# A windowed attention and three convolutions on one core: scores ahead of values in TensorE's order, and a shorter opening

## The chip, the cores and the metric

The kernel runs on one core of one Trainium2 chip. Its time is the device time of one execution in microseconds. Of the kernel before there are three runs: 203.22, 203.52 and 203.56 us, median 203.52 us. A further execution was taken with the profiler. All waits between engines are semaphores written out by hand; each engine works through its own list of instructions in order.

## The reference

The input is eight images of 28 x 28 pixels with 64 channels. Four blocks follow each other, each of the form x = x + block(groupnorm(x)), with 32 groups of two channels:

```python
x = x + attention(_gn(x))     # shifted windows 7x7, 8 heads of 8 channels, relative bias, mask, softmax
x = x + binary_conv(_gn(x))   # 3x3, signs of input and kernel, scaled by a 3x3 mean of |input|
x = x + ternary_conv(_gn(x))  # 3x3, kernel = sign
x = x + gated(_gn(x))         # in-projection, causal conv of 4 taps, silu, gate, out-projection
```

The change touches only the first block. For every window and head it computes

```python
attn = einsum('whnd,whmd->whnm', q * scale, k) + relative_position_bias + attn_mask
out  = einsum('whnm,whmd->whnd', softmax(attn), v)
```

and then a projection of 64 to 64 channels.

## The kernel before

**Tiles.** The images are handled in four pairs (g = 0 to 3), one image in partitions 0 to 63 and one in 64 to 127. An image has 4 x 4 windows. A row R = 4g + r (16 in all) is one row of four windows of an image pair. A row is worked on in two steps of two windows each, k = 2R (even) and k = 2R + 1 (odd); the text calls a step a pair of windows, and there are 32.

**One step of the attention.** *seed(k)* (ScalarE, L553) writes relative bias and mask into one of two PSUM pairs, which alternate by step. *scores(k)* (TensorE, L881) adds q times k on top. *shift(k)* (VectorE, L1292 and L1297) takes the maximum and subtracts it. *turn(k, 0)* and *turn(k, 1)* (TensorE, L892) transpose the result, and *expo(k, j)* (ScalarE, L583) takes the exponential. *values(k)* (TensorE, L912) multiplies with v and gives the sums too. After a row, *weigh(R)* (VectorE, L1306 and L1311) divides, *gather(R)* (TensorE, L925) transposes, *evac_att(R)* (ScalarE, L595, four instructions) brings it out of PSUM, *project(R)* (TensorE, L938) projects, and *residual(R)* (VectorE, L1322) adds it to x.

**What a row needs first.** *proj_qk(R)* (TensorE, L852) computes q and k of a row; *evac_qk(R)* (ScalarE, L562 for the keys `ks`, L563 for the queries `qs`) copies them out; GpSimd's *mask_row* (L224) spreads the keys by head into `kex`, one of two buffers. *proj_v(R)* (TensorE, L862) computes v after q and k have been copied out, since it uses the same PSUM bank; *evac_v(R)* (ScalarE, L573, two instructions) copies it. proj_v(R + 1) and evac_v(R + 1) belong to the even step of row R, for R = 1 to 14; in row 0, proj_v(1) is in the odd step.

**The order of TensorE.** It is written out by hand. L954 loops over steps 0 to 29. A step issues turn(k, 0), turn(k, 1); in an even one proj_qk(R + 2) and project(R - 2), in an odd one gather(R - 1); then values(k - 1); in an even one proj_v(R + 1); and last scores(k + 2). In the odd steps of rows 0, 2, 3, 6, 10 and 14 a small matmul follows, a *mix* (L815, L816) of the moments of a normalisation or (row 3) a sum for the binary convolution (L985). Both write a free part of the bank of q and k. From row 2 on they wait for evac_att of the row before. The mix of row 14 belongs to the binary convolution of the third image pair.

**The order of ScalarE** (L621) in step k: expo(k, 0), expo(k, 1); in an even step evac_qk(R + 2), then evac_v(R + 1); in an odd one evac_att(R - 1); then seed(k + 3). In rows 7 and 11 the odd step ends with *absolutes* (L608), for the binary convolution. seed(k + 3) waits for shift(k + 1), which frees the PSUM pair.

**The order of VectorE** (L1363) in step k: shift(k + 1); in an even step weigh(R - 1) and residual(R - 2); in some odd ones moments, variances and signs for the second block.

**The opening.** *filler(ps, n)* (L821) issues n matmuls of 512 bf16 columns on zeros, whose result nobody reads. Nine of them stand at the very beginning, seven behind the first mix and a small matmul for the bias (L833), four behind proj_qk(0). Then come scores(0), which waits for a first part of the key mask made by VectorE (kex_first) and for `ks`, `qs` and seed(0); proj_v(0); scores(1); proj_qk(1). ScalarE issues seed(0), seed(1), evac_qk(0), evac_v(0), evac_qk(1), seed(2). seed(1) needs the biased mask that GpSimd builds at L365.

After the loop come the last two steps, mixed with the convolutions of the second block, and then the other blocks; nothing of that is edited.

Of the kernel before, what the change touches and what calls it, by code (L numbers as in the profile page):

```python
# [51 lines left out]
def program(nc, x_in, xw_in, cst_in, wts_in, late_in, ker1_in, ker2_in, rel_in, out):  # L52
    ctx = ExitStack()
    with ctx:
# [3 lines left out]
        def bank(name, n=1):  # L58
            return ctx.enter_context(nc.psum_tensor(name, [P, n, 512], F32))
# [13 lines left out]
        def cc(name):  # L73
            a, n = CI[name]
            return cst[:, a:a + n]

        def ww(name):
            t, a, n = WI[name]
            return (wts, late)[t][:, a:a + n]
# [19 lines left out]
        def col(l, g):  # L99
            return l * NG + g  # L100
# [49 lines left out]
        ps_t = [bank("turned0")[:, 0], bank("turned1")[:, 0]]  # L150
# [57 lines left out]
        NP = 2 * NR  # L208
# [318 lines left out]
        def _(act):  # L527
# [7 lines left out]
            def seed(k):  # L535

                R, p = k // 2, k % 2
                c = 2 * (R % NW == NW - 1)
                if k < 2:
                    act.wait_ge(bits_set, 1)  # L540
                    act.wait_ge(ld_rel, 16)
                else:
                    act.wait_ge(sub_done, k - 1)
                if k == 1:
                    act.wait_ge(rel_built, 1)
                if k == 2 * NW - 2:
                    act.wait_ge(rel_built, 3)
                o = ps_s[p][0:WK, :, 0:NH * WT].rearrange("p j (a n) -> p j a n", a=2)
                if p == 0:
                    i = rel[0:WK, c].rearrange("p (j o n) -> p j o n", j=2, o=1).broadcast_to([WK, 2, 2, 4 * WT])  # L550
                else:
                    i = rel[0:WK, c:c + 2].rearrange("p a (j n) -> p j a n", j=2)
                act.activation(o, i, ACT.Identity).then_inc(seeded, 1)  # L553

            def evac_qk(R):

                act.wait_ge(qk_done, R + 1)
                if R > 0:
                    act.wait_ge(kex_ready, R)
                if R == 1:  # L560
                    act.wait_ge(kex_first, 1)
                act.activation(ks[:], ps_qk[:, RT:2 * RT], ACT.Identity, bias=ww("bk")).then_inc(ks_ready, 1)  # L562
                act.activation(qs[:, R % 2], ps_qk[:, 0:RT], ACT.Identity, bias=bqs[:, 0:1], scale=SCALE)\  # L563
                   .then_inc(q_ready, 1)

            def evac_v(R):

                act.wait_ge(v_done, R + 1)
                if R >= 2:
                    act.wait_ge(pv_done, 2 * R - 2)  # L570
                for e in range(2):
                    q = slice(64 * e, 64 * e + WT)
                    last = act.activation(  # L573
                        vsb[q, R % 2].rearrange("p (a n) d -> p a n d", a=NW)[:, :, :, 9 * e:9 * e + HD],
                        ps_qk[q, 0:NW * C].rearrange("p (a n d) -> p a n d", a=NW, d=HD), ACT.Identity)
                last.then_inc(v_ready, 1)
# [32 lines left out]
                               bias=nmr[:, j:j + 1], scale=rstd[:, j:j + 1]).then_inc(ab_ready, 1)  # L609

            seed(0)
            seed(1)
            act.wait_ge(ld_w, 16)
            act.wait_ge(bqs_ready, 1)
            evac_qk(0)
            act.wait_ge(init_dve, 1)
            evac_v(0)
            evac_qk(1)
# [186 lines left out]
        def _(pe):  # L805
# [12 lines left out]
            def filler(ps, n):  # L818

                for _ in range(n):  # L820
                    mm = pe.matmul(ps, idle[:, 0:P], idle[:], start=True, stop=True)  # L821
                return mm
# [8 lines left out]
            pe.wait_ge(ld_w, 16)  # L831

            pe.matmul(ps_o[:, 0:1], ww("wp"), ww("bv"), start=True, stop=True).then_inc(pe_bt, 1)  # L833
            filler(ps_t[1], 7)

            def proj_qk(R):

                pe.wait_ge(xn_ready, R + 1)
                if R > 0:
                    pe.wait_ge(q_ready, R)  # L840
                    pe.wait_ge(ks_ready, R)
                if R > 0:
                    pe.wait_ge(v_ready, max(R - 1, 1))
                if R >= 4:
                    pe.wait_ge(att_ready, R - 3)
                if R >= 3:
                    pe.wait_ge(gn_copied, copied_by(R - 3))
                if R == 6:
                    pe.wait_ge(aw_ready, 1)
                rhs = xn[:, R % 3]  # L850
                for n, name in enumerate(("wq", "wk")):
                    mm = pe.matmul(ps_qk[:, n * RT:(n + 1) * RT], ww(name), rhs, start=True, stop=True)  # L852
                mm.then_inc(qk_done, 1)

            def proj_v(R):

                pe.wait_ge(xn_ready, R + 1)
                pe.wait_ge(q_ready, 1 if R == 0 else min(R + 2, NR))
                pe.wait_ge(ks_ready, 1 if R == 0 else min(R + 2, NR))
                for a in range(NW):  # L860
                    for e in range(2):
                        mm = pe.matmul(ps_qk[64 * e:64 * e + WT, a * C:(a + 1) * C], xn[:, R % 3, a],  # L862
                                       ww("wv")[:, e * C:(e + 1) * C], start=True, stop=True)
                mm.then_inc(v_done, 1)

            def scores(k):
                R, p = k // 2, k % 2
                if p == 0:
                    pe.wait_ge(q_ready, R + 1)
                if k == 0:  # L870
                    pe.wait_ge(kex_first, 1)
                else:
                    pe.wait_ge(kex_ready, R + 1)
                pe.wait_ge(seeded, k + 1)

                for a in range(2):
                    m = (2 * p + a) * WT
                    for j in range(2):
                        for w in range(2):
                            q = slice(64 * j + 32 * w, 64 * j + 32 * w + 32)  # L880
                            mm = pe.matmul(ps_s[p][64 * w:64 * w + WT, j, a * 4 * WT:(a + 1) * 4 * WT],  # L881
                                           qs[q, R % 2, m:m + WT], kex[q, R % 2, :, m:m + WT],
                                           start=False, stop=True, skip_group_check=True)
                mm.then_inc(s_done, 1)

            def turn(k, j):
                pe.wait_ge(sub_done, k + 1)
                if k > 0:
                    pe.wait_ge(exp_done, 2 * k - 1 + j)
                for n in range(4):  # L890
                    h = 8 * j + 2 * n
                    mm = pe.transpose(ps_t[j][0:WK, n * P:n * P + WK],  # L892
                                      d[0:WK, k % 2, h:h + 2, :].rearrange("p a b -> p (a b)")[:, 0:WK],
                                      ident[0:WK, 0:WK])
                mm.then_inc(t_done, 1)
# [47 lines left out]
                return 1 + (R >= 0) + (R >= 2) + sum(R >= NW * g + 2 for g in range(1, NG))  # L943

            proj_qk(0)
            filler(ps_t[1], 4)
            pe.wait_ge(init_dve, 2)
            pe.wait_ge(ld_c, 16)
            scores(0)
# [4 lines left out]
            for k in range(NP - 2):  # L954
                R, p = k // 2, k % 2
                g, r = R // NW, R % NW

                turn(k, 0)
                turn(k, 1)
                if p == 0 and R + 2 < NR:  # L960
                    proj_qk(R + 2)
                if p == 0 and R >= 2:
                    project(R - 2)
                if p == 1 and R >= 1:
                    gather(R - 1)
                if k == 1:
                    proj_v(1)
                if k >= 1:
                    values(k - 1)
                if p == 0 and 0 < R < NR - 1:  # L970
                    proj_v(R + 1)
                if k + 2 < NP:
                    scores(k + 2)
                if p == 1 and (R in (0, 2, 3) or r == 2):
                    if R > 0:
                        pe.wait_ge(att_ready, R)
                    else:
                        pe.wait_ge(v_ready, 2)
                    if R == 0:
                        mix(1, 1, 2, mixed)  # L980
                    if R == 2:
                        mix(2, 2, 3, mixed)
                    if R == 3:
                        pe.wait_ge(asum_ready, 1)
                        pe.matmul(mixed[:, 0:C], cc("ones"), asum[:], start=True, stop=True).then_inc(pe_alpha, 1)  # L985
                    if g > 0 and r == 2:
                        mix(col(1, g - 1), 1, nth(1, g - 1), mixed)
# [628 lines left out]
```

## Time and profile before

| | |
|---|---|
| median of three runs | 203.52 us (203.22 to 203.56) |
| profiled execution, its own time | 203.97 us |
| its span, first to last instruction | 202.2 us |
| granted clock of TensorE, mean | 0.999 |
| TensorE busy | 193.0 us, 95% |
| VectorE busy | 153.1 us, 76% |
| ScalarE busy | 142.6 us, 71% |
| GpSimd busy | 107.7 us, 53% |
| the attention loop (L954) | about 15.8 to 122.2 us |

PE is TensorE's matmul side and PEld its weight load, DVE is VectorE, ACT is ScalarE, POOL is GpSimd. Times count from the first instruction. A matmul's start is recorded and its end modelled, so a distance between two groups on TensorE is best taken from start to start. A group's own "us" includes the drain of its last matmul, which overlaps the next group.

### The profile page before, as it was taken

Reading aid. Unit: us, or ns where it says so; the run is one execution under the profiler, and the core shown is the slowest. Engines: PE = TensorE matmul, PEld = TensorE weight load, DVE = VectorE, ACT = ScalarE, POOL = GpSimd, SP = SyncE. Lnnn points to the kernel's source line nnn. Section 1 sums busy time; section 2 is a strip of 40 time slices with the busy share of each in tenths; the row PEclk is TensorE's granted clock in tenths of the full one; section 3 lists DMA queues with packets and bytes.
Section 4 is the critical chain, followed back from the end, with each engine's and each line's share of the span. In section 5 each row is a group of like instructions: output and inputs, shape, how many; then the busy total and the mean of one; then the engine's idle time right before and its main releaser. Section 6 shows DMA issues by size and latency. Waiting matters only on the chain.

```text
span 202.2 us, 7014 instructions
## 1 busy us (share of the span) xinstructions
PE 193.0 (95%) x2828; PEld 133.9 (66%) x2828; DVE 153.1 (76%) x304; ACT 142.6 (71%) x305; POOL 107.7 (53%) x122
## 2 busy tenths in 40 slices
PE   7889999999999999999999999989999799999994
PEld 2557888888888878878878887746555556443321
DVE  5466689978796877887877997799769638865884
ACT  2148688697787798778888874747467638798691
POOL 0337999967402539932369404942934621565490
PEclk9999999999999999999999999999999999999999
DMA  6980000000000010100010101011033361021114
GB/s 200 433 363 3 3 0 6 3 3 5 0 3 3 3 24 5 43 3 3 3 26 3 43 5 27 4 40 46 3 93 90 77 143 35 20 80 40 44 39 161
DMA packets 6111, 10.77 MB, mean 53 GB/s; under 512 B 960, under 2 KB 5184, under 8 KB 5952
## 3 DMA queue, kind: packets, MB, share of 16 engines
q1 hardware_dynamic: 5648, 9.72, 15.5%
q10 hardware_dynamic: 432, 0.60, 0.9%
q8 instruction: 23, 0.38, 0.8%
q14 instruction: 8, 0.07, 0.1%
HBM read 5.03 MB, written 1.61 MB: 33 GB/s over the span
## 4 chain that ended last, share of the span: by engine, by line
PE 66%; POOL 9%; ACT 7%; issue 6%; DMA 5%; DVE 4%; SPq 2%; POOLq 0%; ACTq 0%; DVEq 0%
PE turned L892 12%; PE scores L881 10%; PE outs L912 10%; PE qkv L862 4%; PE qkv L852 4%; PE turned L1136 3%; PE qkv L1124 3%; PE scores L1023 3%; PE scores L1110 3%; PE scores L1095 2%; PE scores L1111 2%; DMA p<-parts 2%; DMA xw<-xw_in 2%; POOL h L414 2%; PE outs L938 2%
## 5 line engine op out<-in xcount | busy, mean ns | idle before, releaser
L1292 DVE TENSOR_REDUCE mx<-scores 113x16 f32<-113x784 f32 x32 | 30.9, 966 | 6.9 <-PE scores L881 6.6
L373 POOL TENSOR_TENSOR rstd<-ve,mhalf 128x1 f32<-128x1 f32 (+1 forms) x15 | 9.6, 640 | 45.2 <-DVE ve L1258 45.0
L892 PE MATMUL turned<-cst,d 113*113 113x113 f32 x256 | 33.2, 273 | 0.0
L892 PEld LDWEIGHTS turned<-cst,d 113*113 113x113 f32 x256 | 27.9, 178 | 7.7 <-issue 7.7
L224 POOL TENSOR_TENSOR kex<-ks,cst 128x784 f32<-128x784 f32 (+1 forms) x16 | 23.6, 1476 | 16.9 <-ACT ks L562 16.9
L583 ACT ACTIVATE pt<-turned 113x392 f32<-113x392 f32 x64 | 28.5, 496 | 5.7 <-PE turned L892 3.1
L1297 DVE TENSOR_TENSOR d<-scores,mx 113x784 f32<-113x784 f32 x32 | 31.2, 976 | 1.1
L553 ACT ACTIVATE scores<-rel 113x784 f32<-113x784 f32 x32 | 26.2, 818 | 5.9 <-POOL rel L365 3.5
L912 PEld LDWEIGHTS outs<-vsb,pt 113*49 113x49 f32 x1024 | 26.0, 125 | 5.6 <-issue 2.5
L881 PE MATMUL scores<-kex,qs 32*49 32x196 f32 x512 | 28.2, 332 | 0.9 <-DVE kex L224 0.5
L912 PE MATMUL outs<-vsb,pt 113*49 113x18 f32 x1024 | 29.0, 199 | 0.0
L573 ACT ACTIVATE vsb<-qkv 49x256 f32<-49x256 f32 x32 | 12.8, 399 | 15.0 <-PE qkv L862 14.7
L1442 DVE SCALAR_TENSOR_TENSOR su<-scores,late,su 128x392 f32<-128x392 f32 x30 | 16.4, 617 | 4.6 <-ACT su L704 4.6
L263 POOL TENSOR_TENSOR kex<-su,sz 128x392 f32<-128x392 f32 x14 | 14.1, 1029 | 9.1 <-ACT su L718 6.4
L881 PEld LDWEIGHTS scores<-kex,qs 32*49 32x49 f32 x512 | 14.8, 117 | 4.9 <-issue 1.6
L595 ACT ACTIVATE att<-qkv 64x98 f32<-64x98 f32 x64 | 16.2, 253 | 2.2 <-PE qkv L925 1.7
L1023 PE MATMUL scores<-p,w 128*64 128x392 bf16 x144 | 13.4, 334 | 1.2 <-DMA p<-parts 1.2
L852 PE MATMUL qkv<-xn,wts 128*128 128x196 f32 x64 | 13.8, 339 | 0.3 <-ACT vsb L573 0.2
L412 POOL TENSOR_TENSOR h<-ab 128x840 f32<-128x840 f32 x4 | 6.3, 1586 | 12.3 <-ACT ab L608 12.3
L1227 DVE BATCH_NORM_STATS2 st<-x 128x6 f32<-128x392 f32 x24 | 12.4, 558 | 0.2
L1023 PEld LDWEIGHTS scores<-p,w 128*64 128x64 bf16 x144 | 7.8, 109 | 6.3 <-DMA p<-parts 1.6
L852 PEld LDWEIGHTS qkv<-xn,wts 128*128 128x128 f32 x64 | 10.6, 196 | 1.2 <-issue 1.1
(143 smaller groups left out, 377.1 us busy)
## 6 DMA issues: line engine op xcount, KB each, us to landing
p<-parts SPq DMA_DIRECT2D x14, 112.5 KB, 2.3
x<-x_in SPq DMA_DIRECT2D x1, 1568.0 KB, 9.9
out<-xw SPq DMA_DIRECT2D x8, 196.0 KB, 1.9
xw<-xw_in SPq DMA_DIRECT2D x1, 784.0 KB, 6.6
xs<-xs SPq DMA_DIRECT2D x6, 98.5 KB, 2.2
v2x<-v SPq DMA_DIRECT2D x6, 98.0 KB, 2.1
ker<-ker_in SPq DMA_DIRECT2D x2, 288.0 KB, 10.2
p3x<-parts SPq DMA_DIRECT2D x8, 60.0 KB, 2.0
```

What stands on the lines that cost most here:

```text
L224: return engine.tensor_tensor(kex[:, par, :, a * WT:b * WT], ks[:, a * WT:b * WT].rearrange("p (o t) -> p o t", o=1).broadcast_to([P, 4, n ...
L553: act.activation(o, i, ACT.Identity).then_inc(seeded, 1)
L583: act.activation(pt[0:WK, k % 2, j].rearrange("p n (w t) -> p n w t", w=2), ps_t[j][0:WK, :].rearrange("p (n w t) -> p n w t", n=4, w=2)[: ...
L595: last = act.activation(att[64 * w:64 * w + 64, :, b:NW:2].rearrange("p i m j -> p m i j"), ps_qk[64 * b:64 * b + 64, 0:2 * P].rearrange(" ...
L852: mm = pe.matmul(ps_qk[:, n * RT:(n + 1) * RT], ww(name), rhs, start=True, stop=True)
L881: mm = pe.matmul(ps_s[p][64 * w:64 * w + WT, j, a * 4 * WT:(a + 1) * 4 * WT], qs[q, R % 2, m:m + WT], kex[q, R % 2, :, m:m + WT], start=Fa ...
L892: mm = pe.transpose(ps_t[j][0:WK, n * P:n * P + WK], d[0:WK, k % 2, h:h + 2, :].rearrange("p a b -> p (a b)")[:, 0:WK], ident[0:WK, 0:WK])
L912: mm = pe.matmul(ps_o[64 * w:64 * w + WT, 18 * n:18 * n + 18], pt[0:WK, k % 2, j, 2 * a + hp, WT * w:WT * w + WT], vsb[0:WK, R % 2, 2 * n ...
L1023: pe.matmul(ps[64 * w:64 * w + 64, 0:HALF], w2[:, tap], p12[:, g % 2, w, ky + i * HR:ky + (i + 1) * HR, kx:kx + HW], start=(tap == 0), sto ...
L1292: dve.tensor_reduce(top, sc, AXX, ALU.max).then_inc(max_done, 1)
L1297: dve.tensor_tensor(d[0:WK, s].rearrange("p (j m) t -> p j m t", j=2)[:, :, :, 0:WT], sc, top.rearrange("p j (m o) -> p j m o", o=1).broad ...
L1442: dve.scalar_tensor_tensor(out=acc, in0=src, scalar=c, in1=acc, op0=ALU.mult, op1=ALU.add)\
```

## The change

In each step of the loop, scores(k + 2) moves from behind proj_v(R + 1) to before values(k - 1), so that it follows proj_qk and project in an even step and gather in an odd one. The condition `k + 2 < NP` is dropped; it always held. In the opening, the fillers behind the first mix become four instead of seven, those behind proj_qk(0) two instead of four, and on ScalarE evac_qk(0) is issued before seed(1).

```diff
--- before.py
+++ after.py
@@ -609,10 +609,10 @@
             seed(0)
-            seed(1)
             act.wait_ge(ld_w, 16)
             act.wait_ge(bqs_ready, 1)
             evac_qk(0)
+            seed(1)
             act.wait_ge(init_dve, 1)
             evac_v(0)
             evac_qk(1)
@@ -831,7 +831,7 @@
             pe.matmul(ps_o[:, 0:1], ww("wp"), ww("bv"), start=True, stop=True).then_inc(pe_bt, 1)
-            filler(ps_t[1], 7)
+            filler(ps_t[1], 4)
@@ -943,7 +943,7 @@
             proj_qk(0)
-            filler(ps_t[1], 4)
+            filler(ps_t[1], 2)
             pe.wait_ge(init_dve, 2)
             pe.wait_ge(ld_c, 16)
             scores(0)
@@ -965,12 +965,11 @@
                     gather(R - 1)
                 if k == 1:
                     proj_v(1)
+                scores(k + 2)
                 if k >= 1:
                     values(k - 1)
                 if p == 0 and 0 < R < NR - 1:
                     proj_v(R + 1)
-                if k + 2 < NP:
-                    scores(k + 2)
                 if p == 1 and (R in (0, 2, 3) or r == 2):
                     if R > 0:
                         pe.wait_ge(att_ready, R)
```

## Rows read from the trace of the kernel before

**Rows 1.** The page's first part: busy us (share of the span) xinstructions.
```profile
PE 193.0 (95%) x2828; PEld 133.9 (66%) x2828; DVE 153.1 (76%) x304; ACT 142.6 (71%) x305; POOL 107.7 (53%) x122
```

**Rows 2.** TensorE's waits, 16 to 122 us: total us, times, longest.
```profile
PE qkv L862 <- ACT qs L563: 0.7, 2, 0.4
PE scores L881 <- POOL kex L224: 0.4, 1, 0.4
```

**Rows 3.** The chain of waits: start us, us, what.
```profile
52.03 0.68 PE qkv L852 x4
...
122.89 0.81 POOL rstd L373
```

**Rows 4.** Timeline, steps 10 and 11: start us, us, engine, line, operation, tiles.
```profile
52.97 0.91 PE L912 MATMUL outs<-vsb,pt 113*49 113x18 f32 x32
...
53.72 0.63 PE L862 MATMUL qkv<-wts,xn 128*49 128x64 f32 x16
53.93 0.36 DVE L1306 RECIPROCAL rc<-outs 113x32 f32<-113x32 f32 x1 [0.82 <-PE outs L912]
54.29 0.88 PE L881 MATMUL scores<-kex,qs 32*49 32x196 f32 x16
...
54.41 0.81 ACT L573 ACTIVATE vsb<-qkv 49x256 f32<-49x256 f32 x2 [0.92 <-PE qkv L862]
...
55.10 1.05 PE L892 MATMUL turned<-cst,d 113*113 113x113 f32 x8
55.10 0.82 ACT L553 ACTIVATE scores<-rel 113x784 f32<-113x784 f32 x1
...
55.98 0.36 PE L925 MATMUL qkv<-cst,osb 113*128 113x113 f32 x2
56.27 0.91 PE L912 MATMUL outs<-vsb,pt 113*49 113x18 f32 x32
56.37 0.98 DVE L1297 TENSOR_TENSOR d<-scores,mx 113x784 f32<-113x784 f32 x1
56.72 1.04 ACT L595 ACTIVATE att<-qkv 64x98 f32<-64x98 f32 x4
57.11 0.88 PE L881 MATMUL scores<-kex,qs 32*49 32x196 f32 x16
...
57.92 1.05 PE L892 MATMUL turned<-cst,d 113*113 113x113 f32 x8
```

**Rows 5.** Timeline, step 16 (row 8), behind the absolutes.
```profile
74.23 0.91 PE L912 MATMUL outs<-vsb,pt 113*49 113x18 f32 x32
...
74.97 0.44 ACT L563 ACTIVATE qs<-qkv,bqs 128x196 f32<-128x196 f32 x1
...
75.51 0.66 PE L862 MATMUL qkv<-wts,xn 128*49 128x64 f32 x16 [0.37 <-ACT qs L563]
```

**Rows 6.** Timeline, step 13 (row 6), with a mix.
```profile
63.66 1.05 ACT L595 ACTIVATE att<-qkv 64x98 f32<-64x98 f32 x4
...
64.86 0.38 PE L815 MATMUL qkv<-mv,cst 128*128 128x2 f32 x2
```

**Rows 7.** Timeline, the opening.
```profile
1.17 4.02 PE L821 MATMUL scores<-idle 128*128 128x512 bf16 x9 [1.17 <-DVE idle L1263]
...
7.12 3.15 PE L821 MATMUL turned<-idle 128*128 128x512 bf16 x7
...
8.46 0.68 DVE L1284 TENSOR_SCALAR xn<-xw,rstd,nmr 128x196 f32<-128x196 f32 x2 [1.04 <-POOL nmr L376]
...
10.06 1.04 PE L852 MATMUL qkv<-xn,wts 128*128 128x196 f32 x4
10.34 0.83 ACT L553 ACTIVATE scores<-rel 113x784 f32<-113x784 f32 x1 [3.51 <-POOL rel L365]
...
10.94 1.03 PE L821 MATMUL turned<-idle 128*128 128x512 bf16 x4
11.23 0.42 ACT L562 ACTIVATE ks<-qkv,wts 128x196 f32<-128x196 f32 x1
```

## The prediction

> **What bounds the kernel now.** I read the page's busy shares first, then TensorE's waits inside the attention, then the timeline of one pair of steps, and the chain of waits last. TensorE is busy for 95% of the span and no other engine passes 76% [rows 1]. Busy can hide small waits, so the second view matters more: from 16 to 122 us, where the attention loop runs, TensorE waited on another engine only three times. Two of the waits are proj_v on ScalarE's query copy, 0.7 us in total; one is scores on GpSimd's key mask, 0.4 us [rows 2]. The reader is to see two things there: no `turn` waits for VectorE, and no `scores` waits for its seed. A reordering of TensorE's groups in that loop can thus win hardly more than those waits. The chain of waits leaves the loop through the mix of its last odd step and goes on at GpSimd's `rstd` at 122.89 [rows 3]. So a microsecond lost before it is a microsecond at the end: the normalisation of the third batch pair and all of the convolutions come behind it.
>
> **The reordering, step by step.** I take steps 10 and 11 as the pattern and count from the start of one group to the start of the next, since these starts are recorded and the ends modelled. In the even step, values(9) 52.97, proj_v(6) 53.72, scores(12) 54.29, turn(11) 55.10; in the odd one, gather at 55.98, values(10) 56.27, scores(13) 57.11, turn(12) 57.92 [rows 4]. Lengths: values 0.75 before proj_v and 0.84 before scores, proj_v 0.57, scores 0.81, turn and gather together 1.17.
>
> In the new even step, scores(12) starts at 52.97, values(9) at 53.78, proj_v(6) at 54.53, and turn(11) again at 55.10. The sum is the same. What is not the same is when proj_v ends: at 55.10 instead of 54.29.
>
> ScalarE's program is not edited. In an even step it issues two exponentials, evac_qk, evac_v and then the seed of three pairs ahead. evac_v waits for proj_v, so the seed waits behind it. Before, evac_v starts at 54.41, 0.12 after proj_v's successor; the seed starts at 55.10, 0.69 later, and lasts 0.82, to 55.92 [rows 4]. scores(13), which needs it, comes only at 57.11: slack 1.19. After, evac_v starts at 55.22, the seed at 55.91 and ends at 56.73. From a ScalarE end to a TensorE start takes 0.10 (qs ends 74.97+0.44=75.41, proj_v starts 75.51) [rows 5], so scores(13) can start at 56.83. But the new order brings it directly behind gather, at 56.27. **Stall 0.56 us.** The two moves, 0.81 later for the seed and 0.84 earlier for its reader, have used up the slack and more.
>
> It happens at every odd step whose even step has a proj_v: rows of windows 1 to 14, so 14 times, 14 x 0.56 = **+7.84 us**. In row 0 proj_v stands in the odd step and values follows scores there; the seed of pair 3 comes ahead of evac_v, no stall. The even steps don't stall: their seed sits behind the exponentials and evac_att of the odd step. Seed start to evac_att's end is 2.66 (55.10 to 56.72+1.04) [rows 4], and the next seed then has the turn, both projections and so about 2 us of TensorE in front of its reader.
>
> **Two things that follow.** First, five odd steps (rows 2, 3, 6, 10, 14) end with a small matmul into the qkv bank that waits for evac_att. Before, evac_att ends at 63.66+1.05=64.71 and the mix starts at 64.86 without a wait [rows 6]. After, in the times of steps 10 and 11, evac_att ends at 55.91+2.66=58.57, the matmul may start at 58.67, and TensorE is there at 56.83+0.81+0.84=58.48: 0.19 each, 5 x 0.19 = **+0.95 us**.
> Second, the waits of proj_v in rows 8 and 12, behind the `absolutes` on ScalarE, go: values to proj_v took 74.23 to 75.51, 1.28 instead of 0.75 [rows 5], so 0.53 is lost there today (the view says 0.37 idle, because it counts from a modelled end). In the new order ScalarE is 0.81 later against the start of the odd turn, and proj_v is later by the stall 0.56 plus the 0.81 of scores ahead of it, 1.37 less the 0.53 = 0.84. Both meet: no wait is left, 2 x 0.53 = **-1.06 us**.
>
> **VectorE and GpSimd.** The weighing waits for values, now 0.81 later, and shift(12) is queued behind it: reciprocal at 53.93, subtraction ended at 56.37+0.98=57.35, 3.42 later [rows 4]. After: 54.74+3.42=58.16 and 0.10 for the signal, 58.26, against a turn(12) at 58.48 with the stall. It is hidden, by 0.2 us only; without the stall turn(12) would be at 57.92 and wait 0.34. So if the seed weren't late, VectorE would be in part of the rows. That bounds what is hidden here: from 0 to 0.34 a row. GpSimd's key mask keeps its time and its reader in the even step comes 1.3 us earlier, inside 7 us of a row; I take 0, at most 0.4 a time as in rows 2, in the two or three rows where it has other work.
>
> **New neighbours on TensorE.** Scores behind gather, values behind scores, turn behind values don't stand in the trace. The nearest rows are values, which takes 0.75 or 0.84 by what follows [rows 4]. So a change of neighbour is worth up to 0.09 either way, some 28 times: bounds -2.5 to +2.5. I take 0, since groups swap places and the sum of lengths is kept.
>
 evac_qk(0) started 0.29 after that point, at 11.23, right behind seed(1), which ran 10.34 to 11.17; with evac_qk(0) in front it starts at about 10.7, and the keys, mask, scores(0) and all behind move with it: **-0.5 us**. Left behind, seed(1) would have eaten this gain; put behind, behind two evacuations of 0.42 it ends at 10.7+0.84+0.83=12.4, and scores(1) can't start before ks ends at 11.1 plus scores(0) 0.81 plus proj_v 0.57, 12.5: hidden. The two fillers less behind proj_qk(0) cost nothing, since TensorE waits for the key mask there. Bounds of the opening: -1.1 (proj_qk(0) starts that much earlier) to +1.4 (next paragraph but one).
>
> **Sum.** +7.84 +0.95 -1.06 -0.5 = +7.2 us. The profiled execution took 203.97 (span 202.2 and 1.8 around it), so 211.2. The median of the runs shown is 0.45 below that execution, so **210.7 us**.
>
> **Rivals.**
> 1. *The clock rises later.* The filler groups show the two levels: 0.43 and 0.22 for the same instruction [rows 7]. The engine had been at work from 7.12 without a pause when it rose; in the new opening there are five fillers less, and a short pause at 8.9. If it stayed at 1.2 GHz past scores(0) and proj_v(0), their 0.81+0.57 would double: +1.4, so 212.1. For it: the nine fillers at the very start, 4.02 us of them, didn't raise it [rows 7]. Against: proj_qk(0) and two fillers fill the time to about 11. 8%. The Trainium skill (TensorE: Matmul & The Clock Gate, Part 1) has the throttled level as the default that activity releases; by that rule fewer fillers speak against the change.
> 2. *VectorE and the stalls add up.* If the seed's stall is shorter than I think, VectorE's 0.34 takes its place: 13 rows x 0.34 = 4.4, less 1.06 and 0.5: +2.9, so 206.4. For it: the margin between both is 0.2 us. Against: the seed's chain is read from recorded starts. 7%.
> 3. *The stalls don't come, faster.* The one mechanism is ScalarE's place in line: it decides at 1.17 us behind the odd turn. If evac_v and the seed (0.12+0.69+0.82+0.10=1.73) were done by then, by overlapping more than they do now, only the gains would be left: -1.06-0.5, so 202.0. Against: both use the same in-order engine, and today they already overlap by 0.12. The waits of rows 2 allow hardly more than this gain. 6%.
> 4. *More is lost:* stalls that spread to GpSimd's mask and neighbours at the dear end, +2.5 on the sum, 213.2. 9%.
>
> The forecast has 70%. Within 0.2% of before (0.4 us, about what a measurement of this kernel can tell from no change) I see little: 3%, a cancellation. Faster 6%, slower 91%. The range of the likeliest is 209.2 to 212.2 with the neighbours' unknown at about half of its bounds; for 8 in 10 I take 207.8 to 213.0.
>
> **What would show it.** In the profile after: scores waiting for ScalarE's seed in 14 odd steps, about 0.5 us each, between gather and scores; the period of a row 7.5 instead of 6.94; the mix waiting for evac_att; no more waits of proj_v on qs; turn(30) 7 us later and the same distance from there to the end; the first ks at about 10.7. It is wrong if scores starts right behind gather, or if the first wait in the odd steps is turn's on VectorE.

## The result and the profile after

The changed kernel takes 211.06 us (median of four runs, 210.78 to 211.58), the kernel before 203.51 us. The ratio is 1.0379, with a 95% interval of 1.0354 to 1.0404: 7.5 us slower. The forecast was 210.7 us. The profiled execution took 211.10 us, with a span of 209.2 us against 202.2.

The page's first part, as in [rows 1]: TensorE does the same work in a longer span.

```profile
PE 194.3 (93%) x2821; PEld 134.2 (64%) x2823; DVE 151.7 (72%) x304; ACT 142.5 (68%) x305; POOL 107.8 (52%) x122
```

TensorE's waits from 14 to 130 us, total us, times and longest, as in [rows 2]. The two waits of proj_v on `qs` are gone, and scores now waits for ScalarE's seed. It does so 14 times: the view puts two of them, at 43.16 and 89.44, down to GpSimd's mask, but there too scores starts 0.14 behind the end of the seed. The view counts from the modelled end of the matmul ahead, so it shows 0.33 where the way from gather to its successor has grown by 0.42 from start to start (0.71 for 0.29). Take such totals as a pointer to the place and the distance between starts as the price.

```profile
PE scores L881 <- ACT scores L553: 3.9, 12, 0.3
PE scores L881 <- POOL kex L224: 1.0, 3, 0.4
```

The timeline of steps 10 and 11 after the change, the same groups as [rows 4]; start us, us, engine, line. turn(11) starts at 56.90.

```profile
54.77 0.88 PE L881 MATMUL scores<-kex,qs 32*49 32x196 f32 x16
...
55.59 0.91 PE L912 MATMUL outs<-vsb,pt 113*49 113x18 f32 x32
56.34 0.63 PE L862 MATMUL qkv<-wts,xn 128*49 128x64 f32 x16
56.55 0.36 DVE L1305 RECIPROCAL rc<-outs 113x32 f32<-113x32 f32 x1 [2.49 <-PE outs L912]
56.90 1.04 PE L892 MATMUL turned<-cst,d 113*113 113x113 f32 x8
...
57.02 0.81 ACT L573 ACTIVATE vsb<-qkv 49x256 f32<-49x256 f32 x2 [1.73 <-PE qkv L862]
...
57.72 0.82 ACT L553 ACTIVATE scores<-rel 113x784 f32<-113x784 f32 x1
57.98 0.38 PE L925 MATMUL qkv<-cst,osb 113*128 113x113 f32 x2
...
58.69 0.88 PE L881 MATMUL scores<-kex,qs 32*49 32x196 f32 x16 [0.33 <-ACT scores L553]
58.98 0.98 DVE L1296 TENSOR_TENSOR d<-scores,mx 113x784 f32<-113x784 f32 x1
59.34 1.04 ACT L595 ACTIVATE att<-qkv 64x98 f32<-64x98 f32 x4
59.49 0.91 PE L912 MATMUL outs<-vsb,pt 113*49 113x18 f32 x32
...
60.34 1.04 PE L892 MATMUL turned<-cst,d 113*113 113x113 f32 x8
```

Read it along ScalarE. evac_v has waited 1.73 us for proj_v (0.92 before) and starts 0.12 behind the odd turn. The seed follows 0.70 later and ends at 58.54, and scores starts at 58.69. The odd step takes 60.34-56.90 = 3.44 us, where it took 57.92-55.10 = 2.82 [rows 4]: 0.62 more. The even step keeps its 4.12. The 0.62 has two parts. gather itself starts 1.08 behind the turn, where it started 0.88 behind it: it follows evac_v's end (57.02+0.81 = 57.83) by 0.15, since it waits for `v_ready`. The other 0.42 is scores behind gather, for the seed. The seed comes last, so it alone sets when scores starts, and the wait of gather is hidden in it.

The odd step of row 6, which ends with a mix, against [rows 6]: evac_att ends at 67.94 and the mix starts at 67.99.

```profile
66.89 1.05 ACT L595 ACTIVATE att<-qkv 64x98 f32<-64x98 f32 x4
67.05 0.91 PE L912 MATMUL outs<-vsb,pt 113*49 113x18 f32 x32
...
67.99 0.38 PE L815 MATMUL qkv<-mv,cst 128*128 128x2 f32 x2
```

`rstd` of the third image pair starts at 130.03, where it started at 122.89 [rows 3]; from turn(30) to the end it is 79.90 us, before 80.01. So all that the loop loses reaches the end.

```profile
130.03 0.80 POOL L373 TENSOR_TENSOR rstd<-ve,mhalf 128x1 f32<-128x1 f32 x1 [10.32 <-DVE ve L1257]
```

The next table is made from starts of turn in the profiles of all kernels below: the first turn, turn(0) to turn(30), the rest of the span, and the length of single steps. "Odd" is an odd step without a mix (in brackets: one that follows a residual of four pieces, where it differs), "mix" that of row 6.

| kernel | turn(0) at | loop | rest | odd | mix | step 16 |
|---|---|---|---|---|---|---|
| before | 15.77 | 106.39 | 80.01 | 2.82 | 3.29 | 4.66 |
| the change | 15.17 | 114.12 | 79.90 | 3.44 | 4.00 | 4.11 |
| e1, loop only | 14.99 | 114.14 | 79.62 | 3.44 | 4.00 | 4.12 |
| e2, opening only | 14.02 | 106.40 | 79.74 | 2.82 | 3.29 | 4.67 |
| e7, odd steps only | 15.82 | 106.56 | 79.46 | 2.82 | 3.29 | 4.67 |
| e8, even steps only | 15.15 | 111.31 | 79.93 | 3.04 (3.11) | 4.00 | 4.45 |
| e5, seed first | 15.89 | 108.53 | 80.17 | 3.04 (3.11) | 3.50 | 4.11 |
| e6, proj_v before values | 15.29 | 116.54 | 82.24 | 3.49 (3.58) | 4.06 | 4.75 |
| e12, e6 and seed first | 13.99 | 113.36 | 79.86 | 3.33 (3.58) | 3.56 | 4.81 |
| e3, fillers only | 16.48 | 106.38 | 80.18 | 2.82 | 3.29 | 4.66 |
| e4, key copy only | 15.05 | 106.37 | 79.87 | 2.82 | 3.29 | 4.66 |
| e10, key copy, absolutes | 15.69 | 106.12 | 79.55 | 2.82 | 3.29 | 4.11 |
| e11, e10 and other fillers | 15.10 | 106.12 | 79.39 | 2.82 | 3.29 | 4.11 |

Within the loop, step lengths agree to about 0.01 us from kernel to kernel where nothing differs. The opening varies by more than a microsecond. So the loop's parts can be read from one profile each, the opening's only from medians. e6 took 211.88 to 217.92 us, and its ratio below is that of its three fast runs (211.88, 212.99 and 214.98 us). In its profile the granted clock is at half from 132.1 to 138.9 us, behind the loop, so its steps in the table are sound and its "rest" of 82.24 is not to be compared.

### The profile page after: what moved, and what is told of

It is laid out like the page before. It is cut to its first block, busy times and chain, and to the rows that moved or that the text cites. A ratio compares the mean times of both kernels' runs of the same rounds, so it can differ in the third digit from the quotient of the medians.

```text
span 209.2 us, 7002 instructions
## 1 busy us (share of the span) xinstructions
PE 194.3 (93%) x2821; PEld 134.2 (64%) x2823; DVE 151.7 (72%) x304; ACT 142.5 (68%) x305; POOL 107.8 (52%) x122
## 4 chain that ended last, share of the span: by engine, by line
PE 44%; POOL 27%; issue 9%; ACT 7%; DMA 4%; DVE 4%; SPq 2%; POOLq 0%; ACTq 0%; DVEq 0%
PE scores L881 8%; PE outs L912 8%; POOL kex L224 5%; PE turned L892 4%; ACT scores L553 3%; PE qkv L852 3%; PE scores L1022 3%; PE turned L1135 3%; POOL h L414 3%; PE qkv L1123 2%; PE qkv L862 2%; POOL w L429 2%; POOL rstd L373 2%; POOL v L421 2%; POOL v L419 2%
## 5 line engine op out<-in xcount | busy, mean ns | idle before, releaser
L881 PE MATMUL scores<-kex,qs 32*49 32x196 f32 x512 | 29.3, 342 | 5.9 <-ACT scores L553 3.9
L881 PEld LDWEIGHTS scores<-kex,qs 32*49 32x49 f32 x512 | 16.4, 120 | 13.7 <-issue 10.9
L1305 DVE RECIPROCAL rc<-outs 113x32 f32<-113x32 f32 x16 | 5.7, 354 | 20.3 <-PE outs L912 20.3
```

## The experiments

Each ratio is against runs of the kernel before that were made beside it, with medians of 203.45 to 203.59 us.

**The two parts apart: e1 and e2.**

```diff
e1, against the change; e2 is before.py with the same lines the other way round
+            seed(1)
             act.wait_ge(ld_w, 16)
             act.wait_ge(bqs_ready, 1)
             evac_qk(0)
-            seed(1)
...
-            filler(ps_t[1], 4)
+            filler(ps_t[1], 7)
...
-            filler(ps_t[1], 2)
+            filler(ps_t[1], 4)
```

> Scores ahead of values in the loop, opening as before. Theory (ScalarE's seed behind evac_v): +7.5 us on the kernel before, 211.4 to 211.7, odd steps 0.6 us longer than before (3.44 for 2.82). Rival (part of the loss comes from the opening's lower clock): under 211.0.

> The opening of the change alone, loop as before. Theory: 0.3 to 0.8 us faster than before, about 203.0, with ks some 1.5 us or more earlier and part of it given back by scores and proj_v at the lower clock. Rival (the fillers were needed): slower than before, 204 or more.

e1 took 211.24 us, ratio 1.0378 (1.0337 to 1.0420). e2 took 203.05 us, ratio 0.9976 (0.9947 to 1.0004). The loop's order is the whole loss, to 0.02 us in the loop's length. What the opening gives is not told from nothing at this precision.

**Which half of the reordering: e7 and e8.** In the change, scores moves in every step. Here it moves in one kind of step and stays last in the other.

```diff
-                scores(k + 2)
+                if p == 1:          # e8: p == 0
+                    scores(k + 2)
                 if k >= 1:
                     values(k - 1)
                 if p == 0 and 0 < R < NR - 1:
                     proj_v(R + 1)
+                if p == 0:          # e8: p == 1
+                    scores(k + 2)
```

> Changed opening, scores ahead of values in the odd steps only; proj_v ends as early as before, scores(k+3) is wanted as early as in the change. Theory: the seed is ready 0.92 us behind the odd turn and scores wants it at 1.17, so no wait: 203.0. Rival (scores ahead of values is slow in itself, by its new neighbours or by the shorter way to its seed): the odd steps stay 0.3 us or more longer, 207 or more.

> Changed opening, scores ahead of values in the even steps only, so proj_v ends 0.81 late but scores(k+3) keeps 2.0 us. Theory: no wait of scores on the seed. What is left are waits that the seed's stall covers in the change: gather for evac_v 0.2 a row (2.8), the mixes for evac_att 0.55 in five rows (2.75), turn for VectorE 0.1 to 0.3 in some rows (0.4), 0.4 won back in rows 8 and 12: 208.6 in all. Rival (the seed is the only thing late): 202 to 203.

e7 took 203.78 us, ratio 1.0014 (0.9992 to 1.0036); e8 208.77 us, ratio 1.0243 (1.0200 to 1.0286). In e7 scores(k + 3) follows gather as closely as in the change and the odd step is 2.82 us, as before. So in the odd steps neither scores ahead of values nor its new neighbours cost anything by themselves, and in the even steps the length is 4.12 in the change too. What costs is what hangs on the late proj_v. The total is 0.8 above the expectation, outside the loop: turn(0) is at 15.82. This is e7's odd step 11, with the seed done at 56.11 and scores 0.29 behind gather:

```profile
55.29 1.04 PE L892 MATMUL turned<-cst,d 113*113 113x113 f32 x8
55.29 0.82 ACT L553 ACTIVATE scores<-rel 113x784 f32<-113x784 f32 x1
...
56.17 0.36 PE L925 MATMUL qkv<-cst,osb 113*128 113x113 f32 x2
56.46 0.88 PE L881 MATMUL scores<-kex,qs 32*49 32x196 f32 x16
```

In e8 proj_v ends late and scores has its old two microseconds, so it doesn't wait. But the step is still 0.22 longer. gather(R - 1) waits for `v_ready` of the row whose evac_v has just become late: in e8 it starts 1.08 behind the turn instead of 0.88. And the mix waits for evac_att; with both waits the step of row 6 is 0.71 longer. These are the mixes' waits in e8, 14 to 130 us:

```profile
PE qkv L815 <- ACT att L595: 1.6, 4, 0.4
PE qkv L987 <- ACT att L595: 0.4, 1, 0.4
```

A late proj_v so costs 0.2 us a row, and 0.7 in a row with a mix, even where no seed is waited for. The loop of e8 is 4.92 us longer than before, and that of the change 7.73. The stalls don't add up: the seed's, which ends last, hides the others.

**The seed out of the line: e5.** ScalarE's seed goes ahead of evac_v in the even steps.

```diff
-                if p == 0 and 0 < R < NR - 1:
-                    evac_v(R + 1)
                 if p == 1 and R >= 1:
                     evac_att(R - 1)
                 if k + 3 < NP:
                     seed(k + 3)
+                if p == 0 and 0 < R < NR - 1:
+                    evac_v(R + 1)
```

> The change, and on ScalarE in the even steps the seed ahead of evac_v, so that it no longer waits for proj_v. Theory: no wait of scores on a seed; left are gather on evac_v (0.2 a row, 2.8), turn on VectorE in three rows (0.4), and rows 8 and 12 keep their 1.1 gain; with the opening 205.2. Rival (VectorE takes the seed's place, 0.34 in nearly every row, beside the gather): 207 or more. Rival (the seed isn't the cause): 211.

e5 took 206.24 us, ratio 1.0107 (1.0072 to 1.0143). Its loop is 2.14 us longer than before and 5.59 shorter than the change's. No scores waits for a seed. The odd step is 3.04, 0.2 of it gather behind evac_v. VectorE shows only in rows with a residual of four pieces, 0.07 us each. Queueing on ScalarE is thus shown to be the cause of 5.59 of the loop's 7.73 us: the same TensorE order, and the stall gone. The total came out 1.0 above what I expected, though the loop is what the terms give (2.8+0.4-1.1 = 2.1); the opening is what differs (turn(0) at 15.89).

**proj_v early in the changed order: e6, and e12.** Here proj_v stands between scores and values.

```diff
                 scores(k + 2)
-                if k >= 1:
-                    values(k - 1)
                 if p == 0 and 0 < R < NR - 1:
                     proj_v(R + 1)
+                if k >= 1:
+                    values(k - 1)
```

> The change with proj_v ahead of values: order scores, proj_v, values in the even steps. ScalarE's seed is ready 0.89 us behind the odd turn, before scores wants it at 1.17, but values now ends at the odd turn and the weighing on VectorE with it. Theory: scores doesn't wait for its seed; turn in the next even step waits for VectorE, 0.57 us with two residual pieces and 0.82 with four, less where a mix stands before it: 207.9. Rival (VectorE has slack that the trace doesn't show): 203.

The ratio is 1.0482 (1.0428 to 1.0535), about 213.3 us where 207.9 was expected, and the expectation failed: scores waits for its seed 14 times, as in the change. The timeline of e6 shows why. evac_v starts at 57.71, 0.18 behind the end of values, which is where turn(11) starts (57.53); proj_v had ended a microsecond earlier, where values starts (56.72). The releaser named is `outs`:

```profile
56.24 0.66 PE L862 MATMUL qkv<-wts,xn 128*49 128x64 f32 x16
56.72 0.88 PE L912 MATMUL outs<-vsb,pt 113*49 113x18 f32 x32
57.53 1.05 PE L892 MATMUL turned<-cst,d 113*113 113x113 f32 x8
...
57.71 0.81 ACT L573 ACTIVATE vsb<-qkv 49x256 f32<-49x256 f32 x2 [1.76 <-PE outs L912]
```

evac_v(R + 1) overwrites the copy of v that values(2R - 1) reads, and waits for it (`pv_done`). I had left this second wait out. With it the seed can't come early in this order, whatever proj_v does. e12 takes the seed out of the line there too (both edits above).

> As the run with proj_v ahead of values, and ScalarE's seed ahead of evac_v. Theory (evac_v also waits for values, since it overwrites the v that they read; that kept the seed late there): now no scores waits for a seed, and what is left is VectorE, whose weighing starts only when values ends: odd steps 3.33 us with two residual pieces, 3.58 with four, 3.04 where there is none; loop 4.9 us longer than before, 208.3. Rival (the stall there was not the seed's): odd steps stay at 3.49.

e12 took 209.71 us, ratio 1.0308 (1.0275 to 1.0341). No seed is waited for, and the odd steps are 3.33 and 3.58, as expected of VectorE. TensorE's waits of e12:

```profile
PE turned L892 <- DVE d L1296: 1.9, 7, 0.4
PE qkv L862 <- ACT qs L563: 1.3, 2, 0.7
PE qkv L925 <- ACT vsb L573: 1.0, 3, 0.4
```

The total is 1.4 above the expectation. The loop is 6.97 longer than before, 2.1 more than expected. Of this, 1.4 is in steps 16 and 24, 4.81 each, where 4.11 was assumed: proj_v, right behind scores, meets the queries that come late behind the absolutes. The rest wasn't followed up.

**The opening: e3 and e4.** Both against before.py.

```diff
e3
-            filler(ps_t[1], 7)
+            filler(ps_t[1], 4)
...
-            filler(ps_t[1], 4)
+            filler(ps_t[1], 2)
e4
-            seed(1)
             act.wait_ge(ld_w, 16)
             act.wait_ge(bqs_ready, 1)
             evac_qk(0)
+            seed(1)
```

> The kernel before with six fillers for eleven in the opening, seed(1) still ahead of the key copy. Theory: the earlier proj_qk(0) is lost behind seed(1), 203.3 to 203.6. Rival: the fillers alone give the 0.5 us, 203.0.

> The kernel before with the first key and query copy ahead of seed(1), all eleven fillers. Theory: ks starts 0.06 us earlier at most, since proj_qk(0) is done only then: 203.4 to 203.6. Rival: the order on ScalarE gives the gain alone, 203.0.

e3 took 204.77 us, ratio 1.0063 (1.0039 to 1.0088): slower. e4 took 202.42 us, ratio 0.9963 (0.9939 to 0.9987): faster, by 1.0 us by the medians and 0.75 by the ratio. Both expectations missed. In e4's profile TensorE's clock was up for a while (about 4.0 to 7.2 us, by the spacing of the fillers and the granted clock), the first fillers ran faster, and proj_qk(0) started at 8.87. The keys started at 10.51, where [rows 7] has 11.23, and seed(1) only behind them:

```profile
8.87 1.51 PE L852 MATMUL qkv<-xn,wts 128*128 128x196 f32 x4
...
10.51 0.42 ACT L562 ACTIVATE ks<-qkv,wts 128x196 f32<-128x196 f32 x1 [3.13 <-PE qkv L852]
...
11.13 0.83 ACT L553 ACTIVATE scores<-rel 113x784 f32<-113x784 f32 x1
```

In the profile that I had, seed(1) was in nobody's way by chance of that execution. The profile of e1, which has the opening of the kernel before, shows the other case. The fillers behind its first mix are 0.21 apart, so the clock had risen, and proj_qk(0) starts at 8.26. But the keys wait for seed(1), to 10.46:

```profile
8.26 0.93 PE L852 MATMUL qkv<-xn,wts 128*128 128x196 f32 x4 [0.32 <-DVE xn L1283]
...
9.70 0.83 ACT L553 ACTIVATE scores<-rel 113x784 f32<-113x784 f32 x1 [2.10 <-POOL rel L365]
10.46 0.41 ACT L562 ACTIVATE ks<-qkv,wts 128x196 f32<-128x196 f32 x1
```

With the changed opening and a clock that had risen too (e2), proj_qk(0) starts at 8.42 and the keys at 9.47. In e3 proj_qk(0) starts early too (8.64), but the keys follow seed(1), at 10.84, and scores(0), proj_v(0) and scores(1) run at the lower clock (1.49, 1.03 and 1.12 us from start to start).

**A version that beats both: e10, and e11.** e10 is e4 with `absolutes` issued one step later, behind evac_qk, where ScalarE has time. e11 is e10 with fillers 4 and 5.

```diff
                 if p == 0 and R + 2 < NR:
                     evac_qk(R + 2)
+                if p == 0 and R in (2 * NW, 3 * NW):
+                    if R == 2 * NW:
+                        act.wait_ge(init_pool, 3)
+                    absolutes(R // NW - 2)
...
-                if p == 1 and R >= NW and R % NW == NW - 1:
-                    ...
-                    absolutes(R // NW - 1)
```

> The kernel before with the first key and query copy ahead of seed(1), and absolutes issued one step later, behind evac_qk. Theory: 1.0 us from the opening as measured alone, and the two 0.54 us waits of proj_v in rows 8 and 12 go: 201.4, steps 16 and 24 at 4.12. Rival (GpSimd's key mask, queued behind the row sums that wait for absolutes, is now late): no gain or a loss, steps 17 to 19 longer.

> As the run with keys and absolutes, with four fillers behind the first mix and five behind proj_qk(0). Theory (the clock falls because TensorE stands still before scores(0)): granted clock at or near 1.000 in nearly all runs, and proj_qk(0) earlier: 200.9 to 201.4. Rival (the fillers ahead of proj_qk(0) hold the clock): clock of 0.983 to 0.992 in most runs, and 202 or more.

e10 took 202.03 us, ratio 0.9924 (0.9900 to 0.9948), 1.6 us faster than before by the medians. e11 took 203.03 us, ratio 0.9972 (0.9944 to 1.0000), and its mean clock was 0.983 to 0.992 in 7 of 12 runs: its rival came true. In both, step 16 is 4.11, but step 18 grew from 4.12 to 4.53, and the loop gained 0.27 instead of 1.1. e10's rival was right in this: GpSimd masks the keys of row 10 only behind the row sums that wait for absolutes, and the next key copy waits for that buffer.

```profile
77.40 1.83 POOL L414 TENSOR_TENSOR h<-h,ab 128x840 f32<-128x840 f32 x1
...
79.81 1.49 POOL L224 TENSOR_TENSOR kex<-ks,cst 128x784 f32<-128x784 f32 x1
...
81.39 0.42 ACT L562 ACTIVATE ks<-qkv,wts 128x196 f32<-128x196 f32 x1 [0.71 <-POOL kex L224]
81.71 0.42 ACT L563 ACTIVATE qs<-qkv,bqs 128x196 f32<-128x196 f32 x1
82.23 0.66 PE L861 MATMUL qkv<-wts,xn 128*49 128x64 f32 x16 [0.23 <-ACT qs L563]
```

## Why the prediction was right

**The seed's stall.** Forecast 0.56 us in 14 odd steps, measured 0.62 in the nine without a mix. The working held: evac_v 0.12 behind the turn, 0.70 to the seed, 0.82 for it. Its signal took 0.15 to TensorE where I had read 0.10 for another pair. e1, e7 and e5 show it from three sides. What the prediction left out is gather's wait for evac_v, 0.2 us a row. It does no harm to the sum, since the seed ends later. But take the seed's stall away and a loss stays: 4.92 us where evac_att is still late (e8), 2.14 us where it isn't (e5).

**The mixes.** Forecast 0.56+0.19 = 0.75 in five rows, measured 0.71 in row 6. In e5, where the seed's stall is gone, evac_att comes early too, and the step is 3.50.

**Rows 8 and 12.** Forecast -0.53 each, measured 4.66 to 4.11, -0.55.

**The sum of the loop.** Forecast 7.84+0.95-1.06 = 7.73, measured 114.12-106.39 = 7.73. That is closer than the working deserves. The steps with stalls lost some 0.3 more than forecast, and step 1 lost 0.13. Steps 2 and 4 won 0.22 and 0.16, which I hadn't seen: before, proj_v waited there for the query copy, as in rows 8 and 12 but for less. It started 0.94 and 0.91 behind values (24.06 and 31.21), where 0.75 is usual [rows 4], and 0.09 and 0.10 behind the end of `qs`. These waits are too small for the view of [rows 2], which counts from the modelled end of values:

```profile
24.49 0.42 ACT L563 ACTIVATE qs<-qkv,bqs 128x196 f32<-128x196 f32 x1
25.00 0.66 PE L862 MATMUL qkv<-wts,xn 128*49 128x64 f32 x16
...
31.58 0.44 ACT L563 ACTIVATE qs<-qkv,bqs 128x196 f32<-128x196 f32 x1
...
32.12 0.66 PE L862 MATMUL qkv<-wts,xn 128*49 128x64 f32 x16
```

In the new order scores stands ahead of both, and proj_v no longer waits. Beside rows 8 and 12 this is the only place in the loop where the new order helps.

**New neighbours.** Taken as 0 with bounds of 2.5: e7 bears out 0 for the odd steps, and the even step stays at 4.12.

**VectorE.** I said that it hides behind the seed by 0.2 us and would cost up to 0.34 without it. Without the seed's stall (e5) it cost only 0.07 in four-piece rows. There the gather's wait for evac_v holds the next turn back by 0.2, and VectorE comes 0.07 later still: 0.29 in all against 0.34. In the change itself the subtraction ends at 58.98+0.98 = 59.96 and turn(12) starts at 60.34, so it is hidden by 0.28 with 0.10 for the signal. The mechanism was right, and e12, with values last, has it in full.

**The opening.** Forecast -0.5; turn(0) came 0.60 earlier in the profiled execution. That was luck in its parts. proj_qk(0) came 1.8 us and the keys 1.9 us earlier (8.30 and 9.35 against [rows 7]), not 0.5, since the clock had risen early; then it fell, and 1.3 us were given back. That is the price of rival 1, at work beside the forecast: 0.5 for scores(0) (start to start 1.31 for 0.81), 0.46 for proj_v(0) (1.03 for 0.57) and 0.3 for scores(1) (1.43 for 1.13).

What the opening gives depends on when the clock rises, and the profiles show two cases. Where it rises late, the forecast's working holds. In e8, with the changed opening, it rises at about 10.3 us, as in the kernel before: proj_qk(0) starts at 8.87 (forecast 8.97), the keys at 10.60 (10.7), turn(0) at 15.15, 0.62 early. The order of ScalarE is worth little there: e10, which has it and all eleven fillers, has turn(0) at 15.69, 0.08 early. Where the clock rises early, the step of the forecast that fewer fillers bring proj_qk(0) forward fails: it starts 2.65 us behind the first mix with seven fillers (e1, 5.61 and 8.26) and 2.67 with four (e2, 5.75 and 8.42). The gain there is the order of ScalarE: turn(0) at 14.02 (e2) against 14.99 (e1), and in neither did the clock fall again. That seed(1) ahead of the keys costs next to nothing by itself, as I expected of e4, is so only in the first case. One profile of each kernel stands behind this. Whether the two fillers less behind proj_qk(0) cost nothing was not separated from the three less ahead of it.

**The way to the end.** Forecast one to one; turn(30) to the end is 79.90 for 80.01.

## What to carry to other kernels

Before moving a group on one engine, follow its signal into every other engine's queue: what stands behind the instruction that waits for it will be late as well, though nothing on that engine was edited. Count the slack of that follower at both ends, since here one move of scores used up 1.19 us of slack from both sides, 0.81 and 0.84 us. List all waits of each instruction whose time you shift, those that a later semaphore hides included: two of them (gather for `v_ready`, evac_v for `pv_done`) don't show in the trace of before and decided experiments. Where an opening depends on the state of TensorE's clock, one profile is not enough, and a gain of half a microsecond there has to be read from medians.

## What the runs showed of the hardware

TensorE's granted clock in the opening is not the same from execution to execution, and with fewer fillers it falls again more often. These are windows of 2 us of the changed kernel: us, busy of PE, PEld, DVE, ACT and POOL, granted clock, DMA share, GB/s.

```profile
8.00:10.00 2.00, 1.36 (x6) 0.80 (x6) 1.20 (x5) 0.65 (x3) 1.09 (x2) 1.00 1.06 445
10.00:12.00 2.00, 1.36 (x18) 0.78 (x20) 1.53 (x4) 0.81 (x2) 1.57 (x2) 0.72 0.98 415
12.00:14.00 2.00, 2.00 (x32) 1.52 (x32) 1.81 (x2) 0.80 (x2) 0.00 (x0) 0.50 0.99 391
14.00:16.00 2.00, 2.00 (x20) 1.54 (x12) 1.56 (x3) 0.63 (x2) 0.12 (x1) 0.93 0.31 124
```

In these windows the clock is at full level (2.4 GHz) from 8 to about 11 us and at half (1.2 GHz) in the two microseconds from 12. Ahead of the fall TensorE had stood still for 0.96 us before the first mix, 0.96 before proj_qk(0) and 0.97 before scores(0). The mean granted clock of an execution tells in most cases whether it happened. It was 0.992 or lower in 39 of 61 runs of kernels with six fillers (in the profile of e6, one of them, it also fell behind the loop), in 5 of 96 with eleven, and in 7 of 12 of e11 with nine, of which only four stand ahead of proj_qk(0). Moving fillers behind proj_qk(0) didn't help. Which pause decides, if one does, is open. It isn't the one before scores(0) alone: of the seven profiles with a fall in the opening, only the change's has it behind that pause (10.9 us); in e3, e4, e5, e6, e7 and e11 the clock fell at 7.2 to 9.2 us, and scores(0) started at 11.39 or later. Nor is it the one before proj_qk(0) alone: in e4, with eleven fillers, the clock fell at 7.2 us, while the seven in front of proj_qk(0) ran without a pause. What e4 had ahead of them is 1.32 us before the first mix. The granted clock doesn't tell all: from 4 to 10 us it reads 1.00 in the kernel before too, while its seven fillers ran at 0.43 us each [rows 7], half the speed of the four behind them. Take the level from the spacing of equal matmuls there.

The Trainium skill (TensorE: Matmul & The Clock Gate, Part 1) describes the lower level as the default that activity releases, and says that the moment differs between runs of one kernel. The traces agree: the first fillers of every profile are 0.40 to 0.43 us apart, and the rise comes at about 10.5 us in the kernel before and at about 4.1 in the change. turn(0) spreads from 13.99 to 15.89 in kernels with one and the same opening; falls like those above have a part in that.
